# First batch of a post-norm transformer layer: even and odd projections first, low parts on GpSimd, values among the first maxima

## The reference

```python
q, k, v = (split_heads(x @ W.T + b) for W, b in ((Wq, bq), (Wk, bk), (Wv, bv)))
q, k = rope(q) * 16 ** -0.5, rope(k)       # pairs (even, odd) rotated by cos, sin
a = softmax(q @ k.T) @ v
x = layernorm(x + a @ Wo.T + bo)
W1q, W2q = ternary(W1), ternary(W2)        # threshold from mean(abs(W))
out = layernorm(x + relu(x @ W1q.T + b1) @ W2q.T + b2)
```

## Time and profile before

| what | us |
|---|---|
| median of 3 runs | 3234.84 |
| lowest, highest run | 3234.15, 3235.83 |
| the profiled execution, its own time | 3235.67 |
| its span, first to last instruction | 3233.9 |
| busy in the span: PE, DVE, ACT, GpSimd (POOL) | 3190.5, 2970.8, 2528.2, 2157.4 |

### The profile page before, as it was taken

The page is one execution under the profiler, slowest core; times in us unless marked ns, Lnnn a source line. Parts: engine busy times, 40 slices in busy tenths (PEclk is TensorE's granted clock), DMA queues, the critical chain, the costliest instruction groups (busy, mean ns, idle before and its releaser), DMA issues.

```text
span 3233.9 us, 82328 instructions
## 1 busy us (share of the span) xinstructions
PE 3190.5 (99%) x31110; PEld 1769.4 (55%) x31110; DVE 2970.8 (92%) x5710; ACT 2528.2 (78%) x4963; POOL 2157.4 (67%) x2457
## 2 busy tenths in 40 slices
PE   6999999999999999999999999999999999999998
PEld 4545555555555555555555555555555555555555
DVE  7989999999999999999999999999999999999993
ACT  3878888878888888878878877888878878877774
POOL 2676766766766766766767767767767667664455
PEclk7999999999999999999999999999999999999999
DMA  8445354454354454454454454454453453453411
GB/s 214 115 102 110 92 118 106 99 118 110 94 119 107 98 119 105 100 119 99 103 119 103 100 119 102 103 119 100 105 119 96 106 121 91 111 110 73 97 57 35
DMA packets 312712, 342.02 MB, mean 106 GB/s; under 512 B 77372, under 2 KB 259964, under 8 KB 312316
## 3 DMA queue, kind: packets, MB, share of 16 engines
q1 hardware_dynamic: 311740, 335.97, 45.5%
q10 hardware_dynamic: 576, 0.79, 0.2%
HBM read 196.41 MB, written 140.24 MB: 104 GB/s over the span
## 4 chain that ended last, share of the span: by engine, by line
PE 97%; DMA 1%; ACT 1%; DVE 1%; issue 0%; SPq 0%; POOL 0%; ACTq 0%; POOLq 0%; DVEq 0%
PE ob L1049 31%; PE sc L1031 27%; PE job L787 26%; PE ms L1019 11%; PE job L838 0%; ACT prob L1187 0%; PE ms L895 0%; DVE mxp L1619 0%; PE sc L787 0%; DMA qa<-qk_parts 0%; SPq L482 0%; ACT at_st L1194 0%; DMA maxima<-nm 0%; DMA attention<-at_st 0%; DMA os_<-wv 0%
## 5 line engine op out<-in xcount | busy, mean ns | idle before, releaser
L1367 DVE TENSOR_REDUCE mxp<-ms 128x1 f32<-128x512 f32 x4064 | 2602.2, 680 | 193.3 <-PE ms L1019 155.8
L1187 ACT ACTIVATE prob<-sc 128x512 f32<-128x512 f32 x4096 | 2224.9, 597 | 593.7 <-PE sc L1031 562.0
L1019 PE MATMUL ms<-ka,qa 48*128 48x512 f32 x4064 | 1494.4, 440 | 3.3 <-DVE mxp L1619 2.2
L1031 PE MATMUL sc<-qa,ka 50*128 50x512 f32 x4096 | 1495.0, 438 | 2.2 <-ACT prob L1187 0.8
L1031 PEld LDWEIGHTS sc<-qa,ka 50*128 50x128 f32 x4096 | 694.3, 184 | 1020.9 <-ACT prob L1187 862.4
L1049 PE MATMUL ob<-prob,v_sb 128*17 128x512 f32 (+1 forms) x8528 | 1087.3, 582 | 4.5 <-ACT at_st L1194 4.2
L1019 PEld LDWEIGHTS ms<-ka,qa 48*128 48x128 f32 x4064 | 692.7, 184 | 11.7 <-DVE mxp L1367 5.2
L1735 POOL TENSOR_TENSOR ve<-mv,eps_sb 128x2 f32<-128x2 f32 x123 | 24.1, 196 | 571.9 <-DVE mv L1394 571.9
L1756 POOL TENSOR_TENSOR hid_r<-hid,hid_r 128x512 fp32r<-128x512 f32 x248 | 319.6, 1289 | 19.8
L1049 PEld LDWEIGHTS ob<-prob,v_sb 128*17 128x17 f32 x8528 | 141.4, 95 | 314.1 <-issue 314.0
L787 PEld LDWEIGHTS job<-h_t,w_sb 64*128 64x128 f32 x3968 | 271.4, 185 | 17.8 <-issue 1.6
(11 more groups left out here) (251 smaller groups left out, 2740.4 us busy)
## 6 DMA issues: line engine op xcount, KB each, us to landing
qk_parts<-parts SPq DMA_DIRECT2D x122, 512.0 KB, 4.3
ka<-qk_parts SPq DMA_DIRECT2D x378, 128.0 KB, 4.7
qa<-qk_parts SPq DMA_DIRECT2D x378, 128.0 KB, 7.3
attention<-at_st SPq DMA_DIRECT2D x127, 256.0 KB, 4.1
v_sb<-v_ones SPq DMA_DIRECT2D x68, 272.0 KB, 8.4
v_ones<-v_st SPq DMA_DIRECT2D x64, 272.0 KB, 2.4
xn<-x SPq DMA_DIRECT2D x63, 256.0 KB, 4.7
out<-y SPq DMA_DIRECT2D x63, 256.0 KB, 3.9
```

What stands on the lines that cost most here:

```text
L1019: nc.tensor.matmul(ms[upto(b, g, NS1, at) % MS_BANKS][:, :], operand(qa, b, unit_, j, ROWS)[:, qt * P:(qt + 1) * P], operand(ka, b, unit_, ...
L1031: nc.tensor.matmul(sc[upto(b, g, HG * STEPS, n) % SC_BANKS][:, :], operand(ka, b, unit_, j, ROWS + MROWS)[:, tt * P:(tt + 1) * P], operand ...
L1187: nc.scalar.activation(prob[st_ % 2][:, j, :], sc[upto(b, g, HG * STEPS, n) % SC_BANKS][:, :], ACT.Exp).then_inc(s["exp_done"], 1)
L1367: nc.vector.reduce_max(mxp[(b * G + g) % 2][:, kh, j * TT + qt:j * TT + qt + 1], ms[upto(b, g, NS1, at) % MS_BANKS][:, :], AX.X).then_inc( ...
```

## The change

It does four things, all in the prologue. PE runs the even and odd jobs of a quarter with their phases interleaved (e0, o0, e1, o1), and waits between phases only for the own job's phase 0. The value jobs leave the loop over the quarters: those of quarters 0 and 1 come right after it, that of quarter 2 ahead of maximum tile 6, that of quarter 3 ahead of tile 14; tile 21 now also waits until all values are taken. Quarters 1 to 3 write their values to the `job` banks. The low parts of quarters 0 to 2 are made by GpSimd between its memsets, that of quarter 3 by DVE; each quarter has rotation buffers of its own. And the orders of ACT and SP follow: ACT takes the values of quarter 1 after `round_first(3)`, those of quarters 2 and 3 behind one of the two weight sums each, which now stand behind the upper loads of `qa`; SP issues the value stores later, the last two behind the six stores of `first_parts_out`.

```diff
--- before.py
+++ after.py
@@ -154,6 +154,8 @@
 
 
 FIRST_TILES = in_first_unit()
+FIRST_LOW_AT = {4: (0,), 5: (1, 2)}
+FIRST_VALUES_AT = {6: 2, 14: 3}
 
 
 FIRST_ORDER = [*range(0, HALF_TILES, 2), *range(1, HALF_TILES, 2)]
@@ -296,11 +298,11 @@
         ob = pb("ob", [P, NQ])
         job = [pb(f"job{i}", [P, 512]) for i in range(2)]
         free_banks = sc + ms
-        first_banks = {"e": job, "o": sc, "v": ms}
+        first_banks = {"e": job, "o": sc}
         first_x = [xt_sb, xn, xb, y]
         first_r = [xt_r] + [[part[:, 2 * n:2 * n + 2, :] for part in hid_r] for n in range(G - 1)]
         steady_rot = [rot[:, :, i, :] for i in range(2)]
-        first_rot = [steady_rot, [part[:, :, :] for part in hid]] * 2
+        first_rot = [steady_rot] + [[part[:, :, :] for part in pair] for pair in (hid, (ao, ar), (att_t, h1))]
         first_parts = [parts, w1_sb[:, :, :].rearrange("p i (e a t) -> p i e a t", e=2, a=PARTS),
                        w2_sb[:, :, :].rearrange("p (i n) d -> p i (n d)", i=2).rearrange("p i (e a t) -> p i e a t", e=2, a=PARTS), parts]
@@ -344,6 +346,10 @@
         first_loaded = [sem(f"first_loaded{i}") for i in range(G)]
         at_stored = [sem(f"at_stored{i}") for i in range(QH)]
 
+        def v_banks(g):
+
+            return job if g else ms
+
         def upto(b, g, each, n):
 
             return b * (G * each) + (g * each + n)
@@ -405,7 +411,8 @@
 
             cos, sin = table_of(g)
             wait_used(wait, s["roped"], upto(b, g, 2, 0))
-            wait_used(wait, s["parts_done"], upto(b, g, 1, 0) if b else g - 1)
+            if b:
+                wait.wait_ge(s["parts_done"], upto(b, g, 1, 0))
             wait.wait_ge(s["even_taken"], upto(b, g, 2, 2))
             engine.tensor_tensor(into[0], ev_sb[:, :, :], cos, ALU.mult).then_inc(s["products"], 1)
             engine.tensor_tensor(into[1], ev_sb[:, :, :], sin, ALU.mult).then_inc(s["products"], 1)
@@ -723,25 +730,24 @@
-            v_out(0, 0)
-            v_out(0, 1)
             parts_out(0, 0)
-            v_out(0, 2)
             first_heads_out(1)
             sp.wait_ge(s["rows_set"], 2)
             for at in range(2):
                 sp.wait_ge(first_stored[at], 32)
             load_side(sp, 1, 0, 0, slice(0, NQ), s["first_rows"])
+            v_out(0, 0)
             first_heads_out(2)
-            first_parts_out(1, P // G, P)
-            v_out(0, 3)
             first_heads_out(3)
             for at in range(2, G):
                 sp.wait_ge(first_stored[at], 32)
             load_side(sp, 1, 0, 0, slice(NQ, S), qk_loaded[0])
-            for at in range(2, G):
+            v_out(0, 1)
+            for at in range(1, G):
                 first_parts_out(at, P // G, P)
+            v_out(0, 2)
             proj_in(1, 0)
+            v_out(0, 3)
             for at in range(1, G):
                 sp.wait_ge(first_stored[at], 64)
             sp.wait_ge(s["v_stored"], 16 * G)
@@ -772,13 +778,13 @@
             turned = [0]
             begun = {}
 
-            def in_halves(banks, terms, phase, first=True, last=True, tell=None):
+            def in_halves(banks, terms, phase, first=True, last=True, tell=None, met=None):
 
                 if phase == 1 and first:
                     if tell:
                         pe.wait_ge(s[tell[0]], tell[1])
                     else:
-                        pe.wait_ge(s["halves_done"], halves[0])
+                        pe.wait_ge(s["halves_done"], met or halves[0])
...
...
-            def proj_job(b, g, kind, phase, bank_free, x_parts=xt_r, banks=job):
+            def proj_job(b, g, kind, phase, bank_free, x_parts=xt_r, banks=job, met=None):
 
                 if phase == 0 and kind == "e":
                     pe.wait_ge(s["xt_low"], upto(b, g, 1, 1))
@@ -813,7 +819,7 @@
                 last = in_halves([bank[:, columns] for bank in banks[0:2]], terms, phase,
-                                 tell=("v_half", upto(b, g, 1, 1)) if kind == "v" else None)
+                                 tell=("v_half", upto(b, g, 1, 1)) if kind == "v" else None, met=met)
@@ -1097,22 +1103,35 @@
 
             pe.wait_ge(s["ones_set"], 1)
             pe.wait_ge(s["weights_low"], 1)
-            frees = {"e": [], "o": [], "v": []}
+            frees = {"e": [], "o": []}
             for g in range(G):
-                for kind in ("e", "o", "v"):
-                    if (g, kind) == (0, "v"):
-                        pe.wait_ge(s["weights_low"], 2)
-                    frees[kind] = whole(proj_job, 0, g, kind, frees[kind], first_r[g], first_banks[kind])
-
-            for name in ("even_taken", "odd_taken", "v_taken"):
-                pe.wait_ge(s[name], 2 * G)
+                met = {}
+                for kind in ("e", "o"):
+                    proj_job(0, g, kind, 0, frees[kind], first_r[g], first_banks[kind])
+                    met[kind] = halves[0]
+                for kind in ("e", "o"):
+                    frees[kind] = proj_job(0, g, kind, 1, [], first_r[g], first_banks[kind], met[kind])
+
+            def first_values(g):
+
+                free = frees["e"] if g == 1 else [("v_taken", 2 * g)] if g > 1 else []
+                whole(proj_job, 0, g, "v", free, first_r[g], v_banks(g))
+
+            pe.wait_ge(s["weights_low"], 2)
+            first_values(0)
+            first_values(1)
+            pe.wait_ge(s["odd_taken"], 2 * G)
+            pe.wait_ge(s["v_taken"], 2)
 
             pe.wait_ge(s["first_rows"], 16 * QK_DMAS)
             for i, n in enumerate(FIRST_ORDER):
                 if i == HALF_TILES // 2:
                     pe.wait_ge(qk_loaded[0], loads_of(0, 0))
+                if i in FIRST_VALUES_AT:
+                    first_values(FIRST_VALUES_AT[i])
                 if i == HALF_TILES // 2 + len(free_banks):
                     pe.wait_ge(s["abs_summed"], 2)
+                    pe.wait_ge(s["v_taken"], 2 * G)
...
@@ -1315,26 +1334,27 @@
             act.wait_ge(s["ones_set"], 1)
             act.wait_ge(s["bias_scaled"], 1)
             for g in range(G):
-                for name in ("e1", "o1", "v1"):
+                for name in ("e1", "o1"):
                     proj_job(0, g, name, (0, 1), first_banks[name[0]])
-                    if name == "o1":
-                        if g == 0:
-                            split_first(3)
-                        else:
-                            round_first(g - 1)
-                        if g == G - 1:
-                            for at in range(2):
-                                act.wait_ge(first_stored[at], 32)
-                            load_side(act, 0, 0, 0, slice(0, NQ), s["first_rows"])
+                if g == 0:
+                    split_first(3)
+                else:
+                    round_first(g - 1)
+            proj_job(0, 0, "v1", (0, 1), v_banks(0))
+            for at in range(2):
+                act.wait_ge(first_stored[at], 32)
+            load_side(act, 0, 0, 0, slice(0, NQ), s["first_rows"])
             round_first(G - 1)
+            proj_job(0, 1, "v1", (0, 1), v_banks(1))
+            for at in range(2, G):
+                act.wait_ge(first_stored[at], 32)
+            load_side(act, 0, 0, 0, slice(NQ, S), qk_loaded[0])
             for n in range(2):
                 act.wait_ge(s[("w1_loaded", "w2_loaded")[n]], 16)
                 wait_used(act, s["abs_summed"], n)
                 nc.scalar.activation(scratch, prob[n][:, :, :].rearrange("p h q -> p (h q)"),
                                      ACT.Abs, accum_out=asum[:, n:n + 1]).then_inc(s["abs_summed"], 1)
-            for at in range(2, G):
-                act.wait_ge(first_stored[at], 32)
-            load_side(act, 0, 0, 0, slice(NQ, S), qk_loaded[0])
+                proj_job(0, 2 + n, "v1", (0, 1), v_banks(2 + n))
@@ -1607,6 +1627,7 @@
 
                 out_ = first_parts[g]
                 dve.wait_ge(s["first_high"], g + 1)
+                dve.wait_ge(s["parts_done"], g)
                 for e in range(2):
                     last = nc.vector.tensor_tensor(out_[:, :, e, 1, :], first_rot[g][e], out_[:, :, e, 0, :], ALU.subtract)
                 last.then_inc(s["parts_done"], 1)
@@ -1638,14 +1659,12 @@
                 rotate_odd(dve, nc.vector, 0, g)
                 if g == 0:
                     split_first(3)
-                if g > 0:
-                    first_low(g - 1)
                 add_first(g)
-            first_low(G - 1)
             dve.wait_ge(s["consts_loaded"], 96)
             for c in range(KC):
                 nc.vector.tensor_scalar(y2[:, c, 0:P], ones[:, :], bvc_sb[:, c:c + 1], None, ALU.mult
                                         ).then_inc(s["bias_spread"], 1)
+            first_low(G - 1)
             first_maxima(0, HALF_TILES)
             dve.wait_ge(s["mx_cleared"], 1)
             for kind in ("combine", "turn"):
@@ -1936,6 +1955,14 @@
                 for g in range(G):
                     unit(b, g, tail, tail_before)
 
+            def first_low(g):
+
```

(10 more changed lines are left out.)

## The result

The changed kernel takes 3241.53 us in the median of 12 runs (3239.24 to 3244.66), against 3235.24 of 12 runs before. The ratio is 1.0019, 95% interval 1.0010 to 1.0027: 6.3 us slower, where +5.9 was forecast, and just inside the 0.2% that counts as no change. The profiled execution took 3241.24 us, its span is 3239.1 us.

The account below looks back on a forecast made before the run. PE works without pause from its first score tile, so only that tile's start counts. The later path, `load_qk`, adds +5.9 us to the profiled 3235.67, giving 3241.6 (3240.7 against 3234.84); 8-in-10 range 3235.2 to 3243.6.

Parts of the forecast that it names:

- What bounds it: Whole kernel: PE never pauses from its first score tile (72.10 us), so the end moves only as that tile does.
- Step 1: Quarters of the prologue: PE has slack, DVE sets the pace, 3.85 us per quarter if GpSimd cost DVE nothing.
- Step 2: Low parts on GpSimd: taking turns, each subtraction costs DVE 1.29 us, a quarter takes 6.4, quarter 3 is rotated at 37.4.
- starvation: Rival, low parts: GpSimd gets in only once DVE stops, at 30; +11.5 us, 3246.3; chance 10%.
- Step 3: Lower loads: first maximum tile at 41.1 against 40.46 us; last parts at 39.9, their store landed at 43.6.
- Step 4: Upper loads and values: rows at 51.4, 0.9 us ahead, but reductions end at 68.9 against 63.79, +5.1.
- the value chain: Single value buffer, stores behind upper loads and six part stores: landings at 51.9 and 58.2 us hold up tile 21.
- Step 5: Next unit's loads: `load_qk` at 62.3 instead of 56.40, +5.9; maxima's store behind it at 76.1, first score tile 78.0.
- the free one: Rival, low parts: GpSimd costs DVE nothing, both run at their own pace; +1.0 us, 3235.8; chance 20%.
- stores that pass unhindered: Rival, value stores: they drain faster and tile 21 isn't held; some 3 us gained, 3232; chance 6%.

Follow-up runs that it names:

- e1: Changed kernel with the low parts of quarters 0 to 2 made by DVE again instead of GpSimd; 3237.36 us, 1.0008 to the kernel before.
- c2: e10 with the low parts of quarters 0 to 2 on DVE instead of GpSimd; 3232.83 us, 0.9989 to the kernel before.
- e10: e8 with the six qa loads of load_qk(0, 1) moved behind the maxima's store and load; 3236.34 us, 0.9998 to the kernel before.
- e2: Changed kernel with a separate buffer for each quarter's values, so takes don't wait for stores; 3238.85 us, 1.0012 to the kernel before.
- c3: c2 with the stores of values 1 to 3 directly behind the store of quarter 3's heads; 3230.50 us, 0.9983 to the kernel before.
- e8: e2 with all four value jobs right behind the even and odd ones, none among the maximum tiles; 3239.11 us, 1.0009 to the kernel before.
- e6: Changed kernel with the six qa loads of load_qk(0, 1) behind the maxima's store and load; 3240.92 us, 1.0017 to the kernel before.
- e7: Kernel before the change with the six qa loads of load_qk(0, 1) behind the maxima's store and load; 3235.57 us, ratio 0.9999.
- e4: Changed kernel with the twelve loads of load_qk(0, 1) issued by ACT's queue instead of SP's; 3240.42 us, 1.0016 to the kernel before.

## Why the prediction was right

- **What bounds it**: right. Behind the first score tile the profiles show no change that stands out from their scatter of 4.2 us.
- **Step 1**: right. PE has slack (10.23 busy of 14 us), DVE sets the pace. The last sums were set at 37.4 and came at 36.15, with a start 0.9 later than counted.
- **Step 2**: the mechanism is shown (e1, and c2 against e10), its size was off: each GpSimd subtraction costs DVE 1.02 us, not 1.29, so some 0.2 of its 1.26 falls beside a running DVE operation; GpSimd waits too (1.70 instead of 1.26). A quarter takes 5.88, not 6.4. The two cost DVE 2.04 us per quarter, more than the 1.28 that it needs to do the work itself. Neither end of my bounds, no cost and starvation, happened: the low parts came at 23.2, 29.1 and 35.0. The Trainium skill ("SBUF — State Buffer", "Who interferes with whom") states an exclusive lock between a DVE instruction with two SBUF inputs and a GpSimd one that reads SBUF; the long operations on both engines (1.64 to 1.76 and 1.70 us) agree.
- **Step 3**: the last parts came at 38.65 (39.9), their store landed at 42.71 (43.6), 4.0 after its issue, where 3.7 was taken.
- **Step 4**: the landmarks were right (the takes at 51.62 and 58.56, forecast as the landings 51.9 and 58.2, the reductions' end at 69.3, forecast 68.9). What I called the value chain is two things. The single buffer costs the reductions 3.65 us (e2) and by itself nothing that the first score tile shows; the bytes of the stores behind the upper loads cost what reaches it: moving 816 KB of them ahead starts `load_qk` 3.7 us earlier (c3 against c2).
- **Step 5**: `load_qk` at 62.10 (62.3), the maxima's store landed at 75.37 (76.1), the tile at 77.22 (78.0). Right in size, and right that this is the later of two paths (e2, e8). That the loads delay the store is shown by e6 and e7. The reason "the same queue" is at least not the whole of it: in e4 loads of another queue held up `load_v` by 6.0 us and the store was as late. What part the order within SP's queue has stays open.
- **Rivals**: the free one, +1.0, falls with the long DVE operations; starvation likewise; stores that pass unhindered with the waits of 4.05 and 4.40 us.
- The +5.9 against a measured +6.3 in medians and 5.1 in one pair of first score tiles is closer than the executions agree with each other (5.4 us between the changed kernel's fastest and slowest); part of it is luck, errors that cancel (steps 2 and 3 too late, the execution's start late by 0.9). Two small slips in the working: 18.3 + 3 x 6.4 is 37.5, and the lower end of the forecast's own range comes out at 3239.6 by the two terms named (0.5 and 0.6 us less than 3240.7), not 3239.3.

What stays open: e1's median is 4.2 us under the changed kernel's for 1.3 us of its profile's first score tile, and e2's 2.7 for none. Both were profiled in the slowest of their ten executions (3240.26 and 3242.72), so these profiles may not be typical. PE's granted clock rises from 0.50 to 1.00 (1.2 to 2.4 GHz) near 84 us in the changed kernel's profile and near 81 in e1's, 7 and 5 us behind the first score tile, yet e1's stretch behind the tile is no shorter (3162.6 against 3161.9). No run separates these. Nor does any run put PE's old order of phases back: what interleaving is worth apart from taking the values out of the quarters is not shown (a quarter takes 5.52 us before and 4.94 in e1).

## What to carry to other kernels

Before giving GpSimd work beside DVE operations with two SBUF inputs, count DVE's loss: here 1.02 us for each 0.64 us saved. Where two paths end within a microsecond or two of each other (here the store could have landed 1.8 us earlier, 2.7 after its issue instead of 4.5), an edit to one of them can measure as nothing, so judge such edits together: of e2's 3.65 us the first score tile showed nothing until the loads were out of the way. And look at the idle time of the DMA engines, not just of the engines: a store pushed from an idle stretch to behind a load is paid for by whatever waits for the last byte.

## What the runs showed that I had not expected

A load of 272 KB in SP's queue (`load_v`) lands 9.8 us after its issue beside ACT's twelve loads of 128 KB (e4), and 3.8 ahead of them in the changed kernel. The maxima's store, two of 16 KB, lands 4.5 us after its issue with these loads still under way, and 2.7 with half of them moved behind it. They run at 135 to 152 GB/s from 65 to 70 us with the DMA engines fully busy, where the stores and the load of x ahead of them ran at 369. Two windows of the changed kernel, columns as in the earlier trace rows:

```profile
56.00:57.00 1.00, 1.00 (x6) 0.33 (x2) 0.75 (x2) 0.00 (x0) 0.00 (x0) 0.50 1.09 369
68.00:69.00 1.00, 0.00 (x0) 0.00 (x0) 1.00 (x3) 0.00 (x0) 0.00 (x0) 0.50 1.09 152
```
